# Sending each token to its two experts through DRAM, in place of running all eight experts on every token

## The reference

```python
x = x + 0.5 * ffn(layernorm(x))
x = x + attention(layernorm(x))      # 16 heads of 8 channels, ALiBi bias, causal
x = x + 0.5 * ffn(layernorm(x))      # the same weights as the first

def ffn(x):
    xn = layernorm(x) * ln_gamma + ln_beta
    abel = gelu(xn @ abel_w + abel_b)                      # 128 -> 128
    logits = xn @ moe_gate_w + moe_gate_b                  # 128 -> 8 experts
    w, i = top_2(logits); w = softmax(w)                   # w_dense: w at the two, 0 elsewhere
    h = gelu(xn @ ew1[e] + eb1[e])                         # 128 -> 256, every e
    eo = h @ ew2[e] + eb2[e]                               # 256 -> 128
    moe = sum_e w_dense[e] * eo[e]
    moe = moe @ expm(gens[0]) @ expm(gens[1]) @ expm(gens[2])
    gate = sigmoid(concat(abel, moe) @ gc_w + gc_b)
    return x + abel * (1 - gate) + moe * gate
```

## Time and profile before

| | |
|---|---|
| median of 3 runs (lowest to highest) | 982.9 us (982.8 to 985.02) |
| span of the profiled execution | 984.3 us |
| PE, DVE, ACT, POOL busy | 93%, 68%, 48%, 15% |
| mean granted TensorE clock | 0.985 |
| chain that ended last | PE 86%, DVE 10% |

### The profile page before, as it was taken

The page is one execution under the profiler, slowest core; times in us unless marked ns, Lnnn a source line. Parts: engine busy times, 40 slices in busy tenths (PEclk is TensorE's granted clock), DMA queues, the critical chain, the costliest instruction groups (busy, mean ns, idle before and its releaser), DMA issues.

```text
span 984.3 us, 19699 instructions
## 1 busy us (share of the span) xinstructions
PE 911.0 (93%) x6633; PEld 716.6 (73%) x6633; DVE 671.7 (68%) x2328; ACT 470.6 (48%) x791; POOL 147.9 (15%) x127
## 2 busy tenths in 40 slices
PE   1588999999999589999999999999998999999996
PEld 0477999999998456565656565656556999899996
DVE  1686677887775887676767575857424677788865
ACT  6221444454444116556555555555665444445442
POOL 2212022222210301100001010100003122222201
PEclk9999999999999789999999999999999999999998
DMA  8100000000000220202020202020000000000000
GB/s 250 45 2 1 1 1 2 0 0 0 0 1 19 50 49 21 61 11 60 11 58 13 56 14 55 16 53 20 3 1 2 1 12 12 12 11 5 7 12 21
DMA packets 19609, 23.88 MB, mean 24 GB/s; under 512 B 4136, under 2 KB 11088, under 8 KB 19280
## 3 DMA queue, kind: packets, MB, share of 16 engines
q1 hardware_dynamic: 17536, 20.55, 8.8%
q10 hardware_dynamic: 1872, 2.43, 0.8%
q0 software_dynamic: 128, 0.02, 0.0%
HBM read 7.26 MB, written 2.10 MB: 10 GB/s over the span
## 4 chain that ended last, share of the span: by engine, by line
PE 86%; DVE 10%; issue 2%; DMA 1%; ACT 1%; POOL 0%; DVEq 0%; SPq 0%; ACTq 0%
PE bank L1437 23%; PE bank L1565 9%; PE bank L1519 8%; PE bank L1589 8%; PE bank L1276 6%; PE bank L1277 6%; PE bank L1278 6%; PE bank L1496 3%; PE bank L1493 2%; PE pair L1276 2%; DVE arena L894 2%; PE bank L1499 1%; PE pair L1277 1%; PE pair L1278 1%; PE pair L1614 1%
## 5 line engine op out<-in xcount | busy, mean ns | idle before, releaser
L691 ACT ACTIVATE arena<-bank,b_sb 128x512 f32<-128x512 f32 x256 | 169.7, 687 | 213.5 <-PE bank L1278 212.4
L747 ACT ACTIVATE arena<-bank 128x512 f32<-128x512 f32 x320 | 187.1, 599 | 155.0 <-PE bank L1496 99.8
L1437 PEld LDWEIGHTS bank<-w_rot,arena 128*128 128x128 f32 x2048 | 244.6, 192 | 8.4
L1437 PE MATMUL bank<-w_rot,arena 128*128 128x128 f32 x2048 | 247.3, 275 | 0.0
L1061 DVE SCALAR_TENSOR_TENSOR arena<-bank,w_exp,arena 128x128 f32<-128x128 f32 x512 | 143.9, 344 | 96.1 <-PE bank L1437 96.0
L1519 PE MATMUL bank<-kZ,qT 128*128 128x512 f32 (+3 forms) x512 | 153.9, 373 | 10.9 <-DMA kZ<-oT 7.5
L1565 PE MATMUL bank<-qT,kZ 128*128 128x512 f32 (+3 forms) x512 | 157.5, 376 | 1.2 <-DMA qT<-mT_zero 1.2
L1519 PEld LDWEIGHTS bank<-kZ,qT 128*128 128x128 f32 x512 | 87.1, 200 | 52.1 <-issue 24.8
L1174 DVE TENSOR_REDUCE mx<-bank 128x1 f32<-128x512 f32 x128 | 87.9, 686 | 50.8 <-PE bank L1493 50.1
L1276 PE MATMUL bank<-parts,w_hi 128*128 128x512 f32 x256 | 111.2, 434 | 1.2 <-DVEq L917 1.2
L1277 PE MATMUL bank<-parts,w_hi 128*128 128x512 f32 x256 | 101.2, 395 | 0.0
(11 more groups left out here) (188 smaller groups left out, 1235.0 us busy)
## 6 DMA issues: line engine op xcount, KB each, us to landing
qT<-parts SPq DMA_DIRECT2D x42, 128.0 KB
kZ<-parts SPq DMA_DIRECT2D x168, 32.0 KB
out<-x_all SPq DMA_DIRECT2D x8, 256.0 KB, 2.3
arena<-in_bias_k ACTq DMA_DIRECT2D x1, 1024.0 KB, 5.4
arena<-in_bias_q ACTq DMA_DIRECT2D x1, 1024.0 KB, 8.2
arena<-in_ew SPq DMA_DIRECT2D x1, 1024.0 KB, 9.1
qT<-oT SPq DMA_DIRECT2D x6, 128.0 KB
kZ<-oT SPq DMA_DIRECT2D x24, 32.0 KB
```

The costliest lines, as they stand in the source:

```text
L691: nc.scalar.activation(hT[e % 2][:, j, :], ps_up[j][:, :], ACT.Gelu, bias=b1_sb[:, e, j:j + 1]).then_inc(hidden_ok.sem, 1)
L747: nc.scalar.activation(dst, src, ACT.Exp).then_inc(exp_ok.sem, 1)
L1437: last = mm(tile(ps_dn[e % 2], t), hT[e % 2][:, j, t * P:(t + 1) * P], w2_rot[:, e, j, :], start=(j == 0), stop=(j == NJ - 1))
```

## The change

Each ffn layer is cut in three: a gating part for all 8 chunks, one routed expert part over 72 tiles, and a part that adds the results up.

- **Gating** (`gate_stats`, `gate_shift`, `z_`, `transpose_z`, `xn_`, `abel_logits`, `gate_top`, `ranks`, `gate_place`, `send_z`). For chunk g the normalised row of each token (z, 128 values, with its weight and a number that says where its result belongs) is built twice, once for each of its two experts. Small matmuls with triangular ones give each pair its rank within the expert, and POOL scatters the rows to the expert's region in DRAM with 8 indirect DMAs of 128 rows of 528 bytes. For the first layer the 8 chunks lie between the squarings of the set-up. For the second, chunk b - 1 lies in batch b of the attention (constants `AT_G_...`), and the last chunk behind the attention.
- **Tables.** `make_table` works out which expert each of the 72 tiles (8192 / 128 + 8) belongs to and the row of DRAM where it starts. SP fills the gap behind each region with spare rows.
- **Experts** (`experts` on each engine). 72 tiles as 18 quads of four or 36 pairs of two. SP reads four addresses from SBUF into registers and loads the four tiles of a quad; PE transposes them, multiplies by the expert's matrix picked by a register, ACT applies Gelu, PE transposes back and multiplies by the second matrix (132 columns), DVE multiplies by the weight, and POOL scatters each tile's rows to DRAM. The matrices are fp32 now instead of fp32r pairs, biases are added by bf16 matmuls. There are three buffers for the loaded quads (`X_BUFS`) and two for the results (`Y_BUFS`).
- **Sum** (`load_sums`, `sum_pairs`, `gate_tanh`, `finish_x`). The two results of each token are loaded, added, gated and added to x. In the first layer sequences 0 to 2 are finished ahead of the attention and 3 to 7 in its batches (`AT_C_...`), in the second layer all 8 are done at the end.
- The abel branch goes to DRAM (`keep_abel`) and comes back in the expert part (`load_abel`, `abel`). The split of w1 into high and low parts is gone. Loops are unrolled. The constants of the attention's queries and keys come by POOL's DMAs instead of ACT copies.

The core of the diff:

```diff
+TILES = 2 * CH * NT + E
+QUADS = TILES // NT
+PAIRS = TILES // 2
+X_BUFS, Y_BUFS = 3, 2
+AT_G_STATS, AT_G_SHIFT, AT_G_Z, AT_G_Z_T, AT_G_XN = 19, 22, 24, 27, 28
+AT_G_LOGITS, AT_G_TOP, AT_G_ABEL, AT_G_TANH, AT_G_RANK, AT_G_PLACE = 30, 31, 31, 34, 35, 38
+AT_C_SUM, AT_C_TANH, AT_C_X = 25, 27, 29
...
# SP, routed experts
+                for q in range(QUADS):
+                    if q >= X_BUFS:
+                        y_sent_up_to(sp, layer, q - X_BUFS)
+                    starts = nc.values_load_multi_w_load_instructions(
+                        table[0:1, 1, NT * q:NT * (q + 1)], engines=(mybir.EngineType.SP,), min_val=0,
+                        max_val=E * (REGION + P) - P)[1]
+                    for t, start in enumerate(starts):
+                        sp.dma_start(xg[q % X_BUFS][:, t, :],
+                                     z_rows[layer][bass.ds(start, P), :]).then_inc(x_in[q % X_BUFS], 16)
...
# POOL
+            def send_z(g):
+                layer = g // CH
+                wait(pool, placed, g)
+                wait(pool, z_ok, g)
+                for k in range(2):
+                    for t in range(NT):
+                        g_.indirect_dma_start(z_rows[layer], bass.IndirectOffsetOnAxis(place[g % 2][:, k, t:t + 1], 0),
+                                              zz(g)[:, k, t, :], None).then_inc(z_sent[g % 2], 16)
...
+                def send_y(p):
+                    q = p // 2
+                    for i in range(2):
+                        t = 2 * (p % 2) + i
+                        up_to(pool, y_weighted, layer, 2 * p + i + 1)
+                        g_.indirect_dma_start(y_rows[layer],
+                                              bass.IndirectOffsetOnAxis(xg[q % X_BUFS][:, t, Z_PLACE:Z_PLACE + 1].bitcast(I32), 0),
+                                              ys[q % Y_BUFS][:, t, :], None).then_inc(y_sent[q % Y_BUFS], 16)
...
# ACT, gating
+            def z_(g):
...
+                elif g < CH:
+                    z_sent_up_to(act, g - 2)
...
+                for k in range(2):
+                    for t in range(NT):
+                        a_(zz(g)[:, k, t, 0:D], xs(c, t), ACT.Identity, bias=shift[:, t:t + 1],
+                           scale=rstd_g[:, c, 1, t:t + 1]).then_inc(z_ok.sem, 1)
...
# DVE, routed experts
+                    for i in range(2):
+                        t = 2 * (p % 2) + i
+                        v.tensor_scalar(ys[q % Y_BUFS][:, t, :], ps_y[p % 2][:, ROW * i:ROW * (i + 1)],
+                                        xg[q % X_BUFS][:, t, Z_WEIGHT:Z_WEIGHT + 1], None, ALU.mult).then_inc(y_weighted.sem, 1)
...
# PE, routed experts
+                def x_turn(q):
+                    pe.wait_ge(x_in[q % X_BUFS], 16 * NT * (layer * (QUADS // X_BUFS) + q // X_BUFS + 1))
...
+                    for t in range(NT):
+                        last = nc.tensor.transpose(tile(ps_x[q % 2], t), xg[q % X_BUFS][:, t, 0:D], ident[:, :])
...
+                    for i in range(2):
+                        t = 2 * (p % 2) + i
+                        e, into = chosen_e[q][t], ps_up[p % 2][:, HID * i:HID * (i + 1)]
+                        mm(into, tile(xnT[q % 2], t), of_expert(w1, e, 0, HID), start=True, stop=False)
+                        last = mm(into, three_bf[:, :], of_expert(expert_bias, e, 0, HID), start=False, stop=True)
...
+                x_turn(0)
+                x_turn(1)
+                for p in range(PAIRS + 2):
+                    if p < PAIRS:
+                        up(p)
+                    if p % 2 == 0 and p and p // 2 + 1 < QUADS:
+                        x_turn(p // 2 + 1)
+                    if 1 <= p <= PAIRS:
+                        h_turn(p - 1)
+                    if p >= 2:
+                        down(p - 2)
```

More of the change, by code:

```diff
@@ L471, in _ @@
[L471 to L481 removed]
+            g_ = nc.gpsimd
@@ L806, in _ @@
[L806 to L811 removed]
+                elif g < CH:
+                    if g > 1:
+                        wait(act, abel_logits_ok, g - 2)
+                elif g - CH < BATCH - 3:
+                    wait(act, qk_split, g - CH + 3)
+                else:
+                    wait(act, o_projected, min(g - CH, BATCH - 1))
@@ new lines, in _ @@
+            zero_gaps(0)
+            experts(0)
+            gate_tanh(0)
+            for b in range(2):
+                x_high(b)
+                q_k(b)
+                q_high(b)
+                v_k_high(b)
+                gate_tanh(b + 1)
+            maxima(0)
+            over_batches(act, batch)
+            o_evac(BATCH - 1, 3)
+            y_evac(BATCH - 1)
+            g_last = 2 * CH - 1
+            z_(g_last)
+            xn_(g_last)
+            abel_bias(g_last)
+            tanh_gap(g_last)
@@ L814, in _ @@
+            zero_gaps(1)
+            experts(1)
+            for c in range(CH):
+                gate_tanh(CH + c)
         @block.vector
@@ L1270, in _ @@
+            maxima(0)
+            over_batches(dve, batch)
+            for i in range(NT):
+                normalise(BATCH - 1, i)
+            add_out(BATCH - 1)
+            gate_stats(2 * CH - 1)
+            gate_shift(2 * CH - 1)
+            gate_logits(2 * CH - 1)
+            gate_top(2 * CH - 1)
+            gate_place(2 * CH - 1)
+            make_table(1)
+            experts(1)
+            for c in range(CH):
+                sum_pairs(1, c)
+                finish_x(1, c)
         @block.tensor
@@ new lines, in transpose_max @@
+            def transpose_max(b):
+                wait(pe, max_split, b)
+                if b >= 2:
+                    wait(pe, routed, CH + b - 2, 1)
+                    wait(pe, abel_biased, CH + b - 2)
+                else:
+                    wait(pe, k_out, b + 1)
+                for i in range(NT):
+                    last = nc.tensor.transpose(ps_m[0][0:32, i * P:(i + 1) * P],
+                                               mx2[:, i, :, :, :].rearrange("p g a t -> p (g a t)"), ident[:, :])
+                last.then_inc(max_transposed.sem, 1)
@@ new lines, in transpose_y, with project_o @@
+            def transpose_y(b):
+                wait(pe, y_normalised, b)
+                for t in range(NT):
+                    ins = nc.tensor.transpose(tile(ps_m[0], t), yn[:, t, :], ident[:, :])
+                ins.then_inc(y_transposed.sem, 1)
+            def project_o(b):
+                wait(pe, y_out, b)
+                for t in range(NT):
+                    ins = mm(tile(ps_m[1], t), yT[:, t, :], wo_sb[:, :], start=True, stop=True)
+                ins.then_inc(o_projected.sem, 1)
```

2010 lines of the change are left out of this document (1089 added, 921 removed).

## The result

| | us |
| --- | --- |
| kernel before, median | 983.0 (982.8 to 985.0) |
| kernel after, median | 1386.2 (1384.0 to 1389.3) |
| its profiled execution, span | 1382.0 |
| ratio after to before | 1.410, 95% interval 1.407 to 1.413 |

The changed kernel is 41% slower. The forecast was 1328 us, with a range of 1130 to 1490. The page of after, in the same three lines as the earlier trace rows: the span, the clock in 40 slices, the last chain by engine.

The account below looks back on a forecast made before the run. PE bound the old kernel; in the new one each quad was to wait for loads held by earlier scatters. Terms 195 + 294 + 35 + 451 + 27 + 294 + 33 gave 1329 us of span, forecast 1328, range 1130 to 1490.

Parts of the forecast that it names:

- set-up, to the first row loads: Set-up with eight gatings: 195 us until the first loads, six rounds of 18.0 us making 108; bounds 157 and 224.
- attention: Attention: 424 us before, plus 13 of PE's gating work and 14 of queued DVE reductions, 451; bounds 437 and 475.
- The return loop: Expert part: loads of quad q wait for scatters of quad q - 3, so each quad pays the round trip; period 17.1 us.
- L: Expert part: round trip from weighting through scatters, landing and address reading to landed loads, 9.9 us; bounds 7.2 and 14.
- Work between the returns: Expert part: PE's work from return to last down, 7.2 us, between 4.6 at 2.4 GHz and 9.2 at 1.2 GHz.
- Short returns: Rival, expert part: sends of 0.6 us and cheap registers, round trip 7.4, layer 256, kernel 1204 us; chance 0.22.
- the variant with the clock up: Expert part: short returns with the clock staying up, layer 210 us, kernel 1104; within that rival's chance of 0.22.
- Dear returns: Rival, expert part: round trip 12.5 us, PE mostly at 1.2 GHz (8 us), layer 350, kernel 1472; chance 0.17.
- Loads that keep ahead: Rival, expert part: wait at x_turn costs PE nothing, layer 115 us, kernel 971, or 928 with short sends; chance 0.05.
- The signs: Changed profile: PE idle 8 to 9 us before x_turn, 15 times a layer; loads near 195; attention about 27 us longer.
- the squarings hide in it: Set-up: the squarings, 5 us a round, were claimed to hide in the gating cycle of 18.0 us.
- the DVE term: Attention: DVE's reductions that free PE's score banks queue behind gating and sums, 2 us a batch, 14 in all.

Follow-up runs that it names:

- e10: e1 with the three skip operations of a chunk moved from POOL's list to DVE; 1060.7 us, ratio 1.078.
- e2: The changed kernel with 34 useless identity products on PE in front of the wait at each x_turn from quad 3 on; 1306.4 us, ratio 1.328.
- e1: The changed kernel with six buffers for the loaded rows instead of three, abel stores later in SP's list; 1084.7 us, ratio 1.104.
- e4: The changed kernel with the second four of ACT's eight z rows behind the norm, in set-up and attention; 1373.3 us, ratio 1.397.
- e5: e1 and e4 together plus four z buffers instead of two in the set-up; 1081.9 us, repeated at 1012.4 us.
- e6: e1 with DVE taking a chunk's skip product one pair later in its list; 1145.2 us, repeated at 1082.0 us.

## Why the prediction was right

The direction, the mechanism and its place were as forecast. The terms, cut as the prediction cuts them (an expert part goes from the issue of its first row loads, at 230.1 and 1053.9, to the landing of its last scatter, at 523.4 and 1345.9):

| part | predicted | measured |
| --- | --- | --- |
| set-up, to the first row loads | 195 | 230.1 |
| expert part, first and second | 294, 294 | 293.3, 292.0 |
| turn to the attention | 35 | 36.5 |
| attention | 451 | 464.6 |
| turn to the second expert part | 27 | 29.4 |
| sums at the end | 33 | 36.1 |
| sum | 1329 | 1382 |

**The return loop** was right step by step. L was put at 9.9 us. It was 9.3 in the quad shown, and 9.2 to 10.1 in the 15 of the first layer, 9.6 in the mean:

| step of L | predicted | measured, quad shown |
| --- | --- | --- |
| weighting, signal | 0.6 | 0.66 |
| two scatters and landing | 4.3 | 3.53 |
| reading four addresses | 1.0 | 1.34 |
| four loads and landing | 3.8 | 3.74 |

The scatter itself is 0.96 us, 1.27 with the gap to the next, for the 1.2 taken between 0.6 and 1.65. But landing counts from the issue (2.27 us), and the second scatter's 0.96 lies inside it; the prediction put them end to end. The transfers, 0.5 us apart and 2.0 to land, are as the output line of the earlier trace rows had them at 2.3. Work between the returns was 7.4 us in the mean against 7.2, the clock coming back on the way as had been taken, and a period 17.0 against 17.1. PE's 1.45 us a tile, from the earlier trace rows, stand against 1.43 in e10, where nothing else holds it. From the first weighting of the loop (250.2) to the last x_turn (497.7) are 247.5 us (250 predicted), and the rest of the part is 45.8 (44).

The scatter, the reading of the addresses and the work at the mixed clock had each been taken near the middle of far bounds. That all three came out within 0.4 us is in part luck.

On these tensor loads the Trainium skill (DMA: Bandwidth & Descriptors, Latency and other measured facts) gives a floor of about 600 ns. The trace doesn't agree for a load from SBUF on SP: it takes 0.30 us. Nor are there four of them in a quad, as the prediction's estimate had it: one load of 0.30 us is followed by four register operations of 0.15, 1.34 us in all with the gaps, where the estimate made 2.4.

**The rivals.** Short returns failed on the scatter (1.27 us with its gap, for 0.6) and on the addresses (1.34), and the variant with the clock up failed on the clock, which e2 shows to fall in the waits. Two of its figures don't follow from their terms: scatters of 0.6 and an address step of 0.3 make an L of 8.0, not 7.4 (nor 7.2, the lower bound), and 157 + 210 + 35 + 445 + 22 + 210 + 33 is 1112, not 1104. Both lie far from what was measured. Dear returns failed on L and on the work at half clock (7.4 us, not 8). Loads that keep ahead was the case to be built: e1 has it and shows what it was worth. It said 0.4 us of waiting a quad or less would save the change, with POOL's list taken as no limit below 3.7 us a send; with the skip in it POOL was a limit at 1.27. From the first x_turn to the last scatter its 115 us a layer were 137 in e1 and 125 in e10.

**The signs.** PE's idle times in front of x_turn (8.1 to 9.0 us in the first layer), their releaser, the clock and the scatter were as foretold. Two signs were not: the first loads came at 230 us and not near 195, and PE was busy for 93% of the attention, which was 40 us longer, and not for 99% of one 27 us longer.

**Where a term was mis-sized.**
- Set-up, 35 us too low, the largest error. The first scatter came at 69.9 us for the 64 forecast (6 us), six cycles took 135 for 108 (27), and from there to the first row loads were 25 for 23 (2). The cycle was put at 18.0 us and took 22.5. Scatters and landing were right (11.2 us for 11.6). The step that failed is "the squarings hide in it": in the chain above they stand between the logits and DVE's copy of them, 2.0 to 2.7 us, because PE's and DVE's lists have them there. The logits took 2.9 us for 1.4. Their pairs of products are 0.55 us on that chain, where the granted clock was 0.50, and 0.28 near 66 us, at full clock; the prediction had applied the clock to the expert part alone. And ACT's rows and the transposes behind them, put at 1.7 us, took 2.9: ACT writes all eight z rows ahead of the norm, and when e4 let it write four, the transposes at half clock took the others' place.
- Attention, 13.6 too low. PE's idle time was as predicted (30.7 us for 14.8 before, where 14 more were expected), but not by DVE's reductions alone. PE's waits in the attention:

```profile
PE bank L1864 <- ACT arena L952: 8.8, 7, 1.5
PE pair L1839 <- DVE mx L1432: 7.9, 7, 1.8
PE bank L1817 <- DVE mx L1418: 3.4, 8, 1.0
```

  The first, ACT behind its z rows, wasn't in the prediction at all; the other two are the DVE term. What was too small is PE's own work: 433.8 us busy against 409.4, 24 more where 13 were given. A part of it lies in the products that both kernels have. Summed over each line's own times, which overlap, the score products and the masks took 490.8 us for 480.8 before, at the same counts. The granted clock was 0.78 for 0.83 in the first 50 us and 0.99 for 1.00 behind them. e4 gains 4.4 us of busy time without taking any work away. How the rest divides between the clock and the gating itself no run shows.
- Turns and end, 7 us too low together, 3 of them at the end. The windows of the last stage:

```profile
1350.00:1360.00 10.00, 0.00 (x0) 0.00 (x0) 5.29 (x16) 0.59 (x2) 0.00 (x0) 0.50 0.82 236
1360.00:1370.00 10.00, 0.00 (x0) 0.00 (x0) 7.86 (x24) 0.89 (x3) 0.00 (x0) 0.50 0.89 264
```

  I had costed DVE's sums at 3.1 us a chunk. But 784 KB a chunk at a DMA share of 0.82 to 0.89 are what bounds the stage there: two of the chunks waited 5 to 6 us for their loads on the last chain. The transfers had been taken for hidden.
- Expert parts, 1 and 2 us too high. Inside them L was too long by 0.35 us, for the landing that was counted beside the send, and the work between too short by 0.25, so that these two nearly cancelled.

The other errors all point the same way and add up: 1386 lies 4.4% above the forecast.

## What to carry to other kernels

When work is routed through a ring of buffers, write down for each ring what must happen between the last reader and the next write, and at which place of each engine's list, and count how many iterations lie between: three buffers gave no overlap here, and six gave back 301 us. A wait that puts PE to sleep is paid twice, once by itself and once by the clock when PE comes back (here 2.7 us for each wait of 8.5). And when one wait is moved, ask first which engine's list is full: with POOL at its limit, moving the wait gave 3 us and emptying POOL's list gave 24.

## What the runs showed of the hardware

A scatter of 128 rows of 528 bytes holds POOL for 0.96 us (median of 144 in after, the longest 1.42); in a row the next one starts 0.30 us later, and it has landed 2.3 us after its issue. Reading four addresses on SP was one load of 0.30 us and four register operations of 0.15, 1.34 us in all.

In e10 DVE gets three more fp32 operations with two SBUF inputs a chunk, of 0.69 us each, beside these scatters. The scatters' mean went from 1.02 and 1.00 us to 1.06 and 1.01. The Trainium skill (SBUF — State Buffer, SBUF: two separate sides) has a POOL-issued transfer stand still while DVE runs a two-port fp32 copy. The three operations are no such copies, so their price doesn't test that, and no other run here was made to.

The kernels of e5 and e6 took 60 to 70 us more in one set of runs than when they were repeated, in stretches in which ACT, DVE and POOL stand still together and which their traces don't explain, while the kernel before kept its 982.9 us on the same chip. At the place shown the DMA share had been 0.95 for 4 us, and e1 goes through the same transfers, at 0.93 for 4 us, without standing still. What held the engines stays open. It was found only because a prediction was missed in a stage that the edit didn't touch.
